# Gated delta rule and mixture of columns: k and q against the state in one product of 64 columns, small products in whole batches, new order on all engines

## The chip, the cores and the metric

The kernel runs on one core of a Trainium2 chip. It is one program, launched once. The metric is its time on the device in microseconds, the median of several runs. All arithmetic is in fp32.

## What is computed

Two layers follow each other on x of 4 sequences, 2048 tokens and 512 features. The first is a gated delta rule with 16 heads of width 32, which is a recurrence over the tokens:

```
S = S * a_t                                  # per head, S is 32 x 32
kv_mem = k_t S ;  delta = (v_t - kv_mem) * beta_t
S = S + outer(k_t, delta) ;  y_t = q_t S
ctx = rmsnorm(y) * norm_w * silu(gate) ;  x = x + layernorm(ctx @ Wo.T + bo)
```

q, k, v, gate, beta and alpha are projections of the normed x; q and k are normed to length 1, beta is a sigmoid. The second is a mixture: each token picks by its logits one of 16 columns (512 to 128, gelu, back to 512), and layer norms follow.

```
logits = cosine(x, col_emb) + sigmoid(gelu(x @ gate_w1 + b1) @ gate_w2 + b2)
weights = onehot(argmax(logits)) * softmax(logits)
y = (gelu(x @ W_cols + b_cols) * weights) @ proj_w + proj_b + x ;  out = x + layernorm(y)
```

## The kernel before

**Blocks and steps.** The 2048 tokens of each sequence are cut into 32 blocks of 64 tokens, and a block into two chunks of 32 (c = 0, 1). A loop of 35 steps is software pipelined and unrolled. A step makes the projections of the next block (`ahead`), the scan of this block (`chain`), output projection, norms and gate of the previous block (`after`), and routing of the one before that (`late`). Behind the loop stands the mixture itself, from 3020 us on.

**A chunk of the scan.** `state_to_u` multiplies S with the decayed k, on 64 tiles of 32 x 32 (16 groups times 4 heads), into the PSUM tile `uk`. DVE then solves a triangular system in two halves of 16 tokens: `solve_half(c, 0)`, then PE's `first_half_to_u(c)` corrects the second half, then `solve_half(c, 1)`. A solve reads products of pairs of keys times beta, 15 columns of them. Each solve ends in a transpose to `delT`. `change_state` makes the outer products into `su`, and `add_to_state` adds them to the decayed state: S is ready for the next chunk. The outputs are q times S (`state_to_outputs`) plus `chunk_to_outputs`, in the PSUM tile `uq`, copied out by ACT (`copy_outputs`). `key_products(c)` makes the products of keys and of keys with queries, and `decay_products(c)` on DVE writes them as `Ak` and `Aq`.

**Pairs.** SP writes `Ak` to DRAM (`write_rows`) and reads it back, spread over the partitions of each head, in eight transfers (`fetch_pairs(c, j)`), two of them outstanding. POOL multiplies them with beta (`pairs_times_beta(c, j)`: seven operations and then eight). The two buffers `pairs[0]`, `pairs[1]` come free when the solve of the same j is over.

**Small and large products.** On PE an fp32 matmul is two matmul instructions in the trace, so a batch of 64 small products is x128, and half a batch x64. A projection (`project`) is eight instructions for a half, 16 for the pair that fills a bank. `squares_sum`, `decays`, `turn` (transposes), `output_projection`, `gate_hidden`, `gate_logits` and `ranks` are the other large ones. All of them write one of three PSUM banks `work`. `TURNS` lists the uses in the order of PE, and `into` makes PE wait until the earlier use of the bank has been read, by the semaphore in `READ_BY`.

**Order.** The order on each engine is written by hand in its `step`; engines work in order and wait on semaphores (`take`). Routing: `choose_columns` on DVE, `ranks` on PE, `rows_of_tokens` on DVE reads the bank of `rank` and makes `slot`; POOL adds a bias to `xfw` and scatters its rows to DRAM by `slot`. Then POOL adds the residual (`x1`), DVE takes its statistics, ACT norms it into `xfw`, and PE turns that (`turn("xfT", ...)`).

## Time and profile before

| | us |
|---|---|
| median of 3 runs | 3423.63 (3423.21 to 3427.54) |
| profiled execution | 3454.87 |
| its span | 3453.1 |
| granted PE clock, mean | 0.912 of full |
| PE, DVE, POOL, ACT busy | 3006.9, 2357.6, 1913.1, 1824.4 |
| transfers, issue to landing: pairs, `pair_rows`, `xt` | 3.5 to 3.7, 2.3, 5.4 |

A timeline row has the start, the length of a merged run of equal instructions, the engine, the line, what is written and read, and the count; brackets give idle time ahead of it and what ended it. PE's rows overlap by a few hundredths, so that distances are taken from start to start. The lengths of PE's rows are modelled. "issue" is a wait for nothing that the profile shows.

### The profile page before, as it was taken

What the parts mean: (1) busy time and instruction counts of PE and PEld (TensorE: products, weight loads), DVE (VectorE), ACT (ScalarE), POOL (GpSimd) and SP (SyncE); (2) the same over time, 40 slices, a digit from 0 to 9 for tenths busy, and PEclk for the clock granted to TensorE, in tenths of its full rate; (3) what the DMA queues carried; (4) which work ended last, traced back from release to release, by engine and by line L of the source; (5) the groups of instructions that cost most, each with busy time, mean ns of one, the idle gap of its engine ahead of it and who ended that gap; (6) DMA issues with size and microseconds to landing.
All of it is one profiled execution on the core that took longest, in us unless ns stands there. A gap on an engine that the chain in (4) does not pass through costs nothing.

```text
span 3453.1 us, 141658 instructions
## 1 busy us (share of the span) xinstructions
PE 3006.9 (87%) x59368; PEld 2295.4 (66%) x59368; DVE 2357.6 (68%) x10708; ACT 1824.4 (53%) x4154; POOL 1913.1 (55%) x2903
## 2 busy tenths in 40 slices
PE   4899999999999999999999999999999999637774
PEld 4667777777777777777777777777777777414443
DVE  1667666666666766777666666666666677657896
ACT  2355555555555555555555555555555555326664
POOL 1555565455555555555565555555556555416887
PEclk9899999999999999999999999999999999759997
DMA  3544444544444445444444454444445444545773
GB/s 112 132 119 115 113 117 112 124 117 108 118 115 114 117 121 124 112 113 117 115 117 112 124 124 110 114 115 115 116 116 124 124 111 118 142 141 105 132 126 65
DMA packets 350030, 404.87 MB, mean 117 GB/s; under 512 B 31169, under 2 KB 293953, under 8 KB 348881
## 3 DMA queue, kind: packets, MB, share of 16 engines
q1 hardware_dynamic: 332752, 362.10, 42.1%
q0 software_dynamic: 16640, 33.71, 5.4%
q8 instruction: 468, 7.67, 1.0%
q14 instruction: 170, 1.38, 0.1%
HBM read 323.97 MB, written 75.93 MB: 116 GB/s over the span
## 4 chain that ended last, share of the span: by engine, by line
PE 62%; ACT 20%; DVE 11%; issue 4%; POOL 1%; ACTq 1%; DMA 1%; POOLq 0%; SPq 0%; DVEq 0%
PE work L437 25%; PE work L535 7%; PE work L543 3%; PE work L446 3%; DVE uk L1158 3%; DVE Ut L1155 3%; PE su L504 3%; PE work L454 2%; PE uq L497 2%; PE uk L477 2%; PE kkq L469 2%; PE uq L492 2%; PE work L530 2%; PE work L522 2%; PE work L511 2%
## 5 line engine op out<-in xcount | busy, mean ns | idle before, releaser
L437 PE MATMUL work<-xT,w_sb 128*128 128x256 f32 x5120 | 1314.1, 407 | 6.5 <-ACT beta L835 5.1
L992 POOL TENSOR_TENSOR pairs<-pairs,beta 128x240 f32<-128x240 f32 (+14 forms) x1920 | 862.4, 488 | 667.0 <-ACT beta L835 380.9
L437 PEld LDWEIGHTS work<-xT,w_sb 128*128 128x128 f32 x5120 | 996.3, 202 | 183.8 <-issue 31.1
L1158 DVE TENSOR_TENSOR uk<-uk,Ut 128x120 f32<-128x120 f32 (+14 forms) x3840 | 708.6, 226 | 1.1
L1155 DVE TENSOR_TENSOR Ut<-pairs,uk 128x120 f32<-128x120 f32 (+14 forms) x3840 | 688.2, 215 | 5.5 <-POOL pairs L992 5.0
L802 ACT ACTIVATE qraw<-work 128x512 f32<-128x512 f32 x128 | 75.9, 593 | 432.2 <-DVE kq L1171 305.5
L1165 DVE TENSOR_TENSOR S<-Sd,su 128x512 f32<-128x512 f32 x64 | 44.0, 687 | 359.1 <-PE su L504 359.1
L535 PE MATMUL work<-wo_sb,ctxT 128*128 128x512 f32 x512 | 240.6, 613 | 6.3 <-POOL ctxT L1011 6.3
L1003 POOL TENSOR_TENSOR kd<-kd,dec 128x512 f32<-128x512 f32 x64 | 68.0, 1084 | 258.8 <-DVE kd L1237 258.8
L492 PEld LDWEIGHTS uq<-kqd,S 32*32 32x32 f32 x8192 | 90.7, 114 | 156.8 <-ACT oT L792 105.8
L1145 DVE TENSOR_TENSOR uk<-vT,uk 128x128 f32<-128x128 f32 x256 | 62.9, 291 | 187.7 <-PE uk L485 115.8
L492 PE MATMUL uq<-kqd,S 32*32 32x32 f32 x8192 | 105.6, 203 | 95.7 <-ACT oT L792 93.4
L809 ACT ACTIVATE qr<-work 128x512 f32<-128x512 f32 x128 | 75.9, 593 | 193.9 <-PE work L446 191.5
L1017 POOL TENSOR_TENSOR xfw<-xfw,pb_sb 128x1024 f32<-128x1024 f32 x32 | 75.5, 2359 | 175.7 <-DVE slot L1224 175.7
L535 PEld LDWEIGHTS work<-wo_sb,ctxT 128*128 128x128 f32 x512 | 93.7, 193 | 105.4 <-issue 94.8
L1171 DVE TENSOR_TENSOR kq<-qraw,qr 128x512 f32<-128x512 f32 x128 | 136.1, 1082 | 35.0 <-ACT qr L810 35.0
L839 ACT ACTIVATE vT<-work 128x512 f32<-128x512 f32 x64 | 38.2, 597 | 224.5 <-PE work L437 224.5
L981 POOL TENSOR_TENSOR kqd<-kq,eg 128x1024 f32<-128x1024 f32 x64 | 150.3, 2349 | 3.8 <-DVE kq L1171 3.8
L976 POOL TENSOR_TENSOR Sd<-S,eg_end 128x512 f32<-128x512 f32 x64 | 67.9, 1061 | 148.6 <-DVE S L1165 148.6
L446 PE MATMUL work<-qsq,squares 128*128 128x512 f32 x256 | 147.0, 658 | 0.0
L469 PEld LDWEIGHTS kkq<-kq 32*32 32x32 f32 x8192 | 119.1, 105 | 34.1 <-issue 29.8
L1194 DVE TENSOR_TENSOR lt<-work,gb_sb 128x32 f32<-128x32 f32 x32 | 6.1, 191 | 195.7 <-PE work L556 195.7
(249 smaller groups left out, 5970.8 us busy)
## 6 DMA issues: line engine op xcount, KB each, us to landing
pairs<-pair_rows SPq DMA_DIRECT2D x512, 256.0 KB, 3.5
pairs<-pair_rows SPq DMA_DIRECT2D x512, 224.0 KB, 3.7
xt<-in_x SPq DMA_DIRECT2D x66, 256.0 KB, 5.4
pair_rows<-Ak SPq DMA_DIRECT2D x64, 256.0 KB, 2.3
x<-in_x SPq DMA_DIRECT2D x64, 256.0 KB, 4.8
out<-x SPq DMA_DIRECT2D x64, 256.0 KB, 3.7
wo_sb<-xs_rows SPq DMA_DIRECT2D x30, 258.0 KB, 2.9
w_sb<-in_w_in SPq DMA_DIRECT2D x1, 5120.0 KB, 14.9
```

What stands on the lines that cost most here:

```text
L437: mm = pe.matmul(w[:, half * BT:(half + 1) * BT], w_sb[:, f, j * D + hg * P:j * D + (hg + 1) * P], xT[:, f, :], start=(f == 0), stop=(f == ...
L446: pe.matmul(w, blk1, qsq[n % 2][:], start=True, stop=True).then_inc(s["ss_full"], 1)
L469: on_tiles(half, "kkq_full", lambda g, q, q_half: pe.matmul(kkq[q, g], kq[q, g, c, 0, :], kq[q, g, c].rearrange("p a t -> p (a t)"), start ...
L492: on_tiles(half, None, lambda g, q, q_half: pe.matmul(uq[q, g], S[q, g, :], kqd[c][q, g, 1, :], start=(g == 0), stop=True, skip_group_chec ...
L504: on_tiles(half, "su_full", lambda g, q, q_half: pe.matmul(su[q, g, :], kd[c][q, g, :], delT[c][q, g, :], start=True, stop=True))
L535: mm = pe.matmul(w, flat(ctxT[:, hg * B + tb * BL:hg * B + (tb + 1) * BL, :]), wo_sb[:, hg, :], start=(hg == 0), stop=(hg == KD - 1))
L543: mm = pe.matmul(w[:, n * BT:(n + 1) * BT], gw1_sb[:, f, n * P:(n + 1) * P], xfT[:, f, :], start=(f == 0), stop=(f == KD - 1))
L981: link(nc.gpsimd.tensor_tensor(kqd[c][:], kq[:, :, c], eg[:, :, c * C:(c + 1) * C].unsqueeze(2).to_broadcast([P, G, 2, C]), ALU.mult), "kq ...
L992: ins = nc.gpsimd.tensor_tensor(a, a, beta[:, :, t:t + WID[t0]], ALU.mult)
L1155: link(v.tensor_tensor(Ut[:, g, 0:n], pr[:, g], uk[:, g, at:at + 1].to_broadcast([P, G // 2, n]), ALU.mult), "vb_free" if i and (c, j, t0) ...
L1158: link(v.tensor_tensor(uk[:, g, at + 1:at + 1 + n], uk[:, g, at + 1:at + 1 + n], Ut[:, g, 0:n], ALU.subtract), f"pairs_free{j}" if i and t ...
L1171: link(v.tensor_tensor(unit(kq, hp)[:, :, :, 1 - j, :], per_chunk(qraw[n % 2][:]), per_chunk(qr[n % 2][:]), ALU.mult), "kq_ready", hold=(n ...
```

## The change

On PE, `uk` and `uq` become the two halves of one tile `u` over two banks, and `state_to_u` makes k and q times S as one product of 64 columns for each tile; `state_to_outputs` is gone. It now waits for the earlier outputs to be copied. `on_tiles` issues a whole batch of 64 products, where it was halves, and every batch has large products behind it. `chunk_to_outputs(c)` follows in the same step, behind `change_state` and a large product.

ACT takes sigmoids as tanh: the gate is copied out of PSUM, its tanh is taken later, and DVE makes (tanh + 1) times the gate (`norm_w` is halved once); beta is tanh and then an affine. Tanh and gelu share one table, and the table is loaded by hand twice a step. `length_of_normed` moves to the next step, raw q and k are copied straight into `kq`, the norm of the next tokens moves ahead. On DVE `rows_of_tokens` goes behind `solve_half(1, 0)`, the statistics of the next tokens ahead of it, and `decay_products(0)` into the middle of `solve_half(1, 1)`. On POOL `decay_state(1)` and the first seven operations of `pairs_times_beta(1, 1)` go ahead of the additions to `x1`, and the `dec` operations ahead of the scatter. SP loads the next tokens between two fetches, and stores ahead of `write_rows(0)`.

```
 TURNS = [
-    ("logits",), ("xT", 0), ("xT", 1), ("qk", 0), ("rms", 0), ("rms", 1), ("alpha",), ("qk", 1), ("ss", 0),
-    ("qk", 2), ("wo", 0), ("wo", 1), ("rank",), ("ss", 1), ("G", 0), ("G", 1), ("qk", 3), ("ss", 2),
-    ("gate", 0), ("ss", 3), ("gate", 1), ("beta", 0), ("beta", 1), ("xfT", 0), ("xfT", 1), ("v", 0), ("v", 1),
-    ("hid",),
+    ("xT", 0), ("xT", 1), ("rms", 0), ("rms", 1), ("logits",), ("qk", 0), ("qk", 1), ("ss", 0), ("qk", 2), ("ss", 1),
+    ("G", 0), ("G", 1), ("wo", 0), ("wo", 1), ("rank",), ("ss", 2), ("qk", 3), ("gate", 0), ("ss", 3), ("gate", 1),
+    ("beta", 0), ("beta", 1), ("xfT", 0), ("xfT", 1), ("v", 0), ("hid",), ("v", 1),
 ]
 BANK = {use: n % NW for n, use in enumerate(TURNS)}
+BANK["alpha",] = BANK["logits",]
 READ_BY = dict(xT="xT_ready", qk="q_sq_ready", ss="ss_read", alpha="alpha_read", rms="rms_read", G="eg_ready", wo="wo_read",
-               rank="rank_read", gate="gate_used", beta="beta_ready", v="v_read", xfT="xfT_ready", hid="h_ready",
+               rank="rank_read", gate="gate_read", beta="beta_read", v="v_read", xfT="xfT_ready", hid="h_ready",
                logits="logits_read")
...
         qsq = [sb(f"qsq{n}", [P, GU * T]) for n in range(2)]
-        qr = [sb(f"qr{n}", [P, GU * T]) for n in range(2)]
-        sg = sb("sg", [P, GU * T])
+        qr = [sb(f"qr{n}", [P, GU * T]) for n in range(4)]
...
-        uk = ps("uk", [P, G, C])
-        uq = ps("uq", [P, G, C])
+        u = ps("u", [P, G, 2, C])
+        uk, uq = u[:, :, 0, :], u[:, :, 1, :]
...
+                if ahead:
+                    load_tokens(following)
+                if chain:
                     fetch_pairs(1, 1)
-                if ahead:
-                    load_tokens(following)
+                if after:
+                    store(block)
+                if ahead:
                     write_rows(0)
-                if after:
-                    store(block)
-                if ahead:
                     fetch_pairs(0, 0)
...
+            def key_products(c):
+
+                take(pe, "A_ready", free=1, use="kkq")
+                on_tiles(lambda g, q, q_half: pe.matmul(
+                    kkq[q, g], kq[q, g, c, 0, :], kq[q, g, c].rearrange("p a t -> p (a t)"), start=True, stop=True))\
+                    .then_inc(s["kkq_full"], 1)
+
+            def state_to_u(c):
+
+                take(pe, "kqd_ready")
+                take(pe, "uq_free", free=1)
+                take(pe, "S_ready")
+                on_tiles(lambda g, q, q_half: pe.matmul(
+                    u[q, g].rearrange("p a t -> p (a t)"), S[q, g, :], kqd[c][q, g].rearrange("p a t -> p (a t)"),
+                    start=(g % (G // 2) == 0), stop=True, skip_group_check=True)).then_inc(s["uk_full"], 1)
+
...
-                on_tiles(half, None, lambda g, q, q_half: pe.matmul(
-                    uq[q, g], S[q, g, :], kqd[c][q, g, 1, :], start=(g == 0), stop=True, skip_group_check=True))
...
                 if chain:
-                    state_to_u(1, 0)
-                if ahead:
+                    change_state(0)
+                if after:
+                    take(pe, "ctx_ready", 2)
+                    output_projection(0)
+                if chain:
+                    chunk_to_outputs(0)
+                if after:
+                    output_projection(1)
+                if chain:
+                    state_to_u(1)
+                if late:
+                    ranks()
+                if ahead:
...
                     project("gate", 4, 0, 0)
-                if chain:
-                    chunk_to_outputs(0, 0)
-                if ahead:
+                    project("gate", 4, 0, 1)
                     squares_sum(3)
-                    project("gate", 4, 0, 1)
-                if chain:
-                    chunk_to_outputs(0, 1)
-                if ahead:
                     project("gate", 4, 1, 0)
                     project("gate", 4, 1, 1)
...
                 if after:
                     take(pe, "xf_ready", TB)
                     turn("xfT", xfw, 0)
...
+            def load_tanh_gelu():
+                nc.scalar.preload_act_table_set("gelu_and_others")
...
-                take(act, "kq_ready", free=2)
+                j, hp = divmod(n, 2)
                 take(act, "qk_full")
-                nc.scalar.activation(qraw[n % 2][:], bank("qk", n), ACT.Copy)
+                nc.scalar.activation(unit(kq, hp)[:, :, :, 1 - j, :], per_chunk(bank("qk", n)), ACT.Copy)
...
+            def copy_gate(p, hp):
+
+                take(act, "gate_full")
+                link(nc.scalar.activation(flat(unit(silu[1 - p], hp)), bank("gate", hp), ACT.Copy), "gate_read", hold=True)
+
+            def gate_tanh(p, hp):
+
+                nc.scalar.activation(gate_t[hp], flat(unit(silu[1 - p], hp)), ACT.Tanh, scale=0.5).then_inc(s["gate_ready"], 1)
+
+            def beta_sigmoid(hp):
+
+                b = flat(unit(beta, hp))
+                take(act, "beta_full")
+                link(nc.scalar.activation(b, bank("beta", hp), ACT.Tanh, scale=0.5), "beta_read", hold=True)
+                link(nc.scalar.activation(b, b, ACT.Identity, scale=0.5, bias=half[:]), "beta_ready")
...
+                    copy_gate(p, 1)
+                    take(act, "x_mv_ready")
+                    token_norm(x_rn, x_mv)
+                    norm_tokens(xn, xt, x_rn, "xn_ready")
                 if after:
                     take(act, "x1_mv_ready")
                     token_norm(x1_rn, x1_mv)
                     norm_tokens(xfw, x1, x1_rn, "xf_ready")
...
+                load_tanh_gelu()
                 if ahead:
                     if chain:
                         take(act, "vb_free")
-                    link(sigmoid("beta", 0, flat(unit(beta, 0))), "beta_ready")
-                    link(sigmoid("beta", 1, flat(unit(beta, 1))), "beta_ready")
+                        take(act, "pr_ready", 8)
+                    beta_sigmoid(0)
+                    gate_tanh(p, 0)
+                    gate_tanh(p, 1)
+                    beta_sigmoid(1)
+                if after:
+                    copy_turned("xfT", xfT, 0)
+                    copy_turned("xfT", xfT, 1)
+                if ahead:
                     copy_values(0)
...
                 load_ln_exp()
+                if chain:
+                    copy_outputs(1)
+                if ahead:
+                    take(act, "gate_used", 2)
+                if chain:
+                    square_outputs(0)
+                    square_outputs(1)
                 if ahead:
                     copy_values(1)
-                    take(act, "x_mv_ready")
...
+            def pairs_times_beta(c, j, parts=(0, 1)):
+
+                for n in parts:
...
+                if ahead:
+                    for hp in range(2):
+                        take(pool, "gT_ready")
+                        d = flat(unit(dec, hp))
+                        link(nc.gpsimd.tensor_tensor(d, d, gT[hp], ALU.subtract))
+                        by_chunk = d.rearrange("p (n t) -> p n t", t=C)
+                        link(nc.gpsimd.tensor_tensor(by_chunk, by_chunk, mask[:].unsqueeze(1).to_broadcast([P, GU * NC, C]), ALU.add),
+                             "diff_ready")
...
+                if chain:
+                    decay_state(p, 1)
+                    pairs_times_beta(1, 1, (0,))
                 if late:
                     pool.wait_ge(s["scat_done"], added)
...
                 if chain:
-                    decay_state(p, 1)
-                    pairs_times_beta(1, 1)
+                    pairs_times_beta(1, 1, (1,))
...
-                    link(v.tensor_tensor(uk[:, g, h], uk[:, g, h], beta[:, g, th], ALU.mult), behind=1)
+                for i, g in enumerate(turns):
+                    link(v.tensor_tensor(uk[:, g, h], uk[:, g, h], beta[:, g, th], ALU.mult),
+                         "vb_free" if i and (c, j) == (NC - 1, 1) else None, behind=1, hold=True)
 
                 for t0 in range(CS - 1):
+                    if t0 in between:
+                        between[t0]()
                     if t0 in PARTS:
                         take(dve, "pr_ready")
...
                     solve_half(0, 0)
                     decay_products(1)
-                    for c in range(NC):
-                        link(v.transpose(kd[c][:], kq[:, :, c, 0, :]), "kt_ready")
+                if after:
...
                     take(dve, "corr_full")
                     solve_half(0, 1)
+                if ahead:
+                    scale(0)
                 if late:
                     choose_columns()
-                if ahead:
-                    take(dve, "kqd_ready", 2, free=2)
...
+                    for hp in range(2):
+                        take(dve, "g_copied")
+                        link(v.transpose(gT[hp], flat(unit(dec, hp))), "gT_ready")
                 if late:
                     weigh_columns()
                 if after:
...
                     token_stats(y, y_mv, 1, "y_mv_ready")
+                if chain:
+                    take(dve, "uk_full")
+                    solve_half(1, 0)
                 if late:
                     rows_of_tokens()
-                if chain:
-                    add_to_state()
                 if ahead:
                     scale(1)
-                    take(dve, "g_copied")
-                    link(v.transpose(gT[0], gsb[0]), "gT_ready")
-                    take(dve, "g_copied")
-                    link(v.transpose(gT[1], gsb[1]), "gT_ready")
-                if chain:
-                    take(dve, "uk_full")
-                    solve_half(1, 0)
-                if ahead:
                     scale(2)
                     scale(3)
-                    take(dve, "gate_ready")
-                    link(v.tensor_tensor(flat(unit(silu[1 - p], 0)), bank("gate", 0), sg[:], ALU.mult), "gate_used")
                 if after:
                     for tb in range(TB):
                         take(dve, "x1_ready")
                         token_stats(x1, x1_mv, tb, "x1_mv_ready")
                 if ahead:
                     take(dve, "dec_ready", 2)
+                if chain:
+                    take(dve, "corr_full")
+                    solve_half(1, 1, {PARTS[1]: lambda: decay_products(0)} if ahead else {})
+                elif ahead:
                     decay_products(0)
```

Order on PE, in a full step around the second `state_to_u` (L477 before, L474 now). Before:

```order
L446 MATMUL work<-qsq,squares 128x512 [waits wo_read,q_sq_ready]
L522 MATMUL work<-squares,xt 128x128 [waits wo_read,lax_ready]
L522 MATMUL work<-squares,xt 128x128 x3
L522 MATMUL work<-squares,xt 128x128 [waits rank_read]
L522 MATMUL work<-squares,xt 128x128 x3
L477 MATMUL uk<-kqd,S 32x32 [waits S_ready,kqd_ready]
L477 MATMUL uk<-kqd,S 32x32 x31
L437 MATMUL work<-xT,w_sb 128x256 [waits ss_read]
L437 MATMUL work<-xT,w_sb 128x256 x3
L477 MATMUL uk<-kqd,S 32x32 x32
L437 MATMUL work<-xT,w_sb 128x256 x4
```

Now:

```order
L474 MATMUL u<-kqd,S 32x64 [waits S_ready,uq_free,kqd_ready]
L474 MATMUL u<-kqd,S 32x64 x63
L558 MATMUL work<-ohs,squares 128x32 [waits eg_ready,oh_ready]
L561 MATMUL work<-ohs,squares 128x16
L564 MATMUL work<-ohs,squares 128x16 x2
L444 MATMUL work<-qsq,squares 128x512 [waits wo_read,q_sq_ready]
L435 MATMUL work<-xT,w_sb 128x256 [waits wo_read]
L435 MATMUL work<-xT,w_sb 128x256 x7
L435 MATMUL work<-xT,w_sb 128x256 [waits rank_read]
L435 MATMUL work<-xT,w_sb 128x256 x7
```

Before, two half batches had a projection between them, and `ranks` stood ahead. Now the batch is whole and 64 columns wide; `ranks` and a sum of squares follow, and the second projection behind them (the gate) waits for `rank_read`, which comes from `rows_of_tokens` on DVE.

Order on DVE around `rows_of_tokens` (its five rows begin with `lt<-work,rows`). Before:

```order
L1219 TENSOR_TENSOR lt<-work,rows 128x32 [waits rank_full]
L1221 TENSOR_TENSOR rows<-rows,work 128x16 [waits dve_step]
L1222 TENSOR_TENSOR lt<-lt,oh 128x32
L1223 TENSOR_REDUCE slotf<-lt 128x2 [waits dve_step]
L1224 CAST slot<-slotf 128x2 [waits dve_step]
L1165 TENSOR_TENSOR S<-Sd,su 128x512 [waits Sd_ready,su_full]
L1171 TENSOR_TENSOR kq<-qraw,qr 128x16x32 [waits q_r_ready]
L1271 STREAM_TRANSPOSE qraw<-qsq 128x512 [waits g_copied,kq_ready]
L1273 STREAM_TRANSPOSE ctxT<-ctxT 128x512 [waits g_copied]
L1145 TENSOR_TENSOR uk<-vT,uk 128x8x16 [waits uk_full]
```

Now:

```order
L1145 STREAM_TRANSPOSE delT<-u 128x512 [waits pairs_free0]
L1215 TENSOR_TENSOR lt<-work,rows 128x32 [waits rank_full]
L1217 TENSOR_TENSOR rows<-rows,work 128x16 [waits dve_step]
L1218 TENSOR_TENSOR lt<-lt,oh 128x32
L1219 TENSOR_REDUCE slotf<-lt 128x2 [waits dve_step]
L1220 CAST slot<-slotf 128x2 [waits dve_step]
L1156 TENSOR_TENSOR kq<-kq,qr 128x16x32 [waits q_r_ready] x3
L1103 BN_STATS stats<-x 128x6 [waits x1_ready]
L1104 BN_AGGR x_mv<-stats 128x2 [waits dve_step]
L1103 BN_STATS stats<-x 128x6 [waits x1_ready,dve_step]
L1104 BN_AGGR x_mv<-stats 128x2 [waits dve_step]
L1127 TENSOR_TENSOR u<-vT,u 128x8x16 [waits corr_full,dec_ready]
```

Before, the slots came ahead of the update of S, and so ahead of the solve that begins with `uk<-vT,uk`. Now they come behind that solve's last transpose, and the statistics of `x1` and `solve_half(1, 1)` behind them.

Order on POOL from the wait for the slots. Before:

```order
L1017 TENSOR_TENSOR xfw<-xfw,pb_sb 128x2x512 [waits slot_ready]
L1019 DMA xs_rows<-xfw,slot 67712x516 [waits pool_step]
L1019 DMA xs_rows<-xfw,slot 67712x516
L1025 TENSOR_TENSOR dec<-qsq,qraw 128x512 [waits gT_ready]
L1027 TENSOR_TENSOR dec<-dec,mask 128x512 [waits pool_step]
L1030 TENSOR_TENSOR dec<-ctxT 128x512 [waits gT_ready]
L1032 TENSOR_TENSOR dec<-dec,mask 128x512 [waits pool_step]
L1039 TENSOR_TENSOR x<-x,y 128x512 [waits zn_ready,xres_loaded,scat_done]
L1039 TENSOR_TENSOR x<-x,y 128x512 [waits zn_ready]
L976 TENSOR_TENSOR Sd<-S,eg_end 128x512 [waits S_ready]
L992 TENSOR_TENSOR pairs<-pairs,beta 128x16x15 [waits pairs_in101,pairs_in100]
```

Now:

```order
L1008 TENSOR_TENSOR xfw<-xfw,pb_sb 128x2x512 [waits slot_ready]
L1010 DMA xs_rows<-xfw,slot 67712x516 [waits pool_step]
L1010 DMA xs_rows<-xfw,slot 67712x516
L959 TENSOR_TENSOR Sd<-S,eg_end 128x512 [waits S_ready]
L975 TENSOR_TENSOR pairs<-pairs,beta 128x16x15 [waits pairs_in101,pairs_in100]
L975 TENSOR_TENSOR pairs<-pairs,beta 128x16x14
L975 TENSOR_TENSOR pairs<-pairs,beta 128x16x13
L975 TENSOR_TENSOR pairs<-pairs,beta 128x16x12
L975 TENSOR_TENSOR pairs<-pairs,beta 128x16x11
L975 TENSOR_TENSOR pairs<-pairs,beta 128x16x10
L975 TENSOR_TENSOR pairs<-pairs,beta 128x16x9
L1022 TENSOR_TENSOR x<-x,y 128x512 [waits zn_ready,xres_loaded,scat_done]
```

The two additions `x<-x,y` stood ahead of `Sd` and of the pair products; now `Sd` and seven pair products stand between the scatter and them.

## Rows read from the trace of the kernel before

**Rows 1.** The page, busy time of each engine (share of the span) and instructions.
```profile
PE 3006.9 (87%) x59368; PEld 2295.4 (66%) x59368; DVE 2357.6 (68%) x10708; ACT 1824.4 (53%) x4154; POOL 1913.1 (55%) x2903
```

**Rows 2.** One line's instructions, L1165: duration in ns, first and last start.
```profile
L1165 DVE TENSOR_TENSOR S<-Sd,su x64: 669/687/689, 127.1 to 3015.0; 128x512 f32<-128x512 f32 x64
```

**Rows 3.** Timeline of PE, 1500 to 1610: start, length (us), line, operation [idle before <-releaser].
```profile
1506.24 0.41 PE L565 MATMUL work<-ohs,squares 128*128 128x32 f32 x2
...
1507.16 1.10 PE L446 MATMUL work<-qsq,squares 128*128 128x512 f32 x2
...
1523.22 3.72 PE L437 MATMUL work<-xT,w_sb 128*128 128x256 f32 x16
...
1541.34 1.08 PE L492 MATMUL uq<-kqd,S 32*32 32x32 f32 x64 [2.94 <-ACT oT L792]
1543.88 1.12 PE L454 MATMUL work<-squares,xfw 128*128 128x128 f32 x4 [1.46 <-ACT beta L835]
1544.79 3.23 PE L437 MATMUL work<-xT,w_sb 128*128 128x256 f32 x8
...
1559.22 0.75 PE L477 MATMUL uk<-kqd,S 32*32 32x32 f32 x64
...
1563.06 1.07 PE L553 MATMUL work<-ceT,xfT 128*128 128x16 f32 x8 [0.96 <-issue]
...
1569.10 0.38 PE L497 MATMUL uq<-Aq,delT 32*32 32x32 f32 x21 [1.20 <-issue]
...
1573.06 1.99 PE L469 MATMUL kkq<-kq 32*32 32x64 f32 x128
...
1606.02 0.44 PE L477 MATMUL uk<-kqd,S 32*32 32x32 f32 x23 [0.48 <-issue]
1606.39 1.99 PE L437 MATMUL work<-xT,w_sb 128*128 128x256 f32 x8
```

**Rows 4.** Waits of PE in the whole run: us in total, times, longest.
```profile
PE uq L492 <- ACT oT L792: 93.4, 31, 3.4
...
PE uk L477 <- issue: 26.0, 52, 1.7
```

**Rows 5.** Timeline of PE in the last step, which has no projections.
```profile
2950.06 2.12 PE L469 MATMUL kkq<-kq 32*32 32x64 f32 x78 [2.43 <-issue]
```

**Rows 6.** Timeline of DVE, 1500 to 1610.
```profile
1507.64 0.16 DVE L1219 TENSOR_TENSOR lt<-work,rows 128x32 f32<-128x32 f32 x1
...
1582.80 0.49 DVE L1145 TENSOR_TENSOR uk<-vT,uk 128x128 f32<-128x128 f32 x2 [1.27 <-PE uk L485]
...
1592.07 0.72 DVE L1160 STREAM_TRANSPOSE delT<-uk 128x512 f32<-128x512 f32 x1
```

**Rows 7.** Timeline of POOL, 1500 to 1600.
```profile
1508.61 2.35 POOL L1017 TENSOR_TENSOR xfw<-xfw,pb_sb 128x1024 f32<-128x1024 f32 x1 [5.63 <-DVE slot L1224]
...
1513.70 1.28 POOL L1025 TENSOR_TENSOR dec<-qsq,qraw 128x512 f32<-128x512 f32 x1
...
1518.88 2.51 POOL L1039 TENSOR_TENSOR x<-x,y 128x512 f32<-128x512 f32 x2
1521.34 1.06 POOL L976 TENSOR_TENSOR Sd<-S,eg_end 128x512 f32<-128x512 f32 x1
...
1544.39 3.99 POOL L992 TENSOR_TENSOR pairs<-pairs,beta 128x240 f32<-128x240 f32 x7 [12.38 <-ACT beta L835]
```

**Rows 8.** Timeline of ACT, 1500 to 1600.
```profile
1541.94 1.28 ACT L835 ACT_TABLE_LOAD   x1
1543.23 1.09 ACT L835 ACTIVATE beta<-work 128x512 f32<-128x512 f32 x2
...
1559.82 0.29 ACT L771 ACTIVATE nsc<-x_mv,eps 128x2 f32<-128x2 f32 x1
...
1562.61 1.52 ACT L752 ACTIVATE xn<-xt,x_rn 128x512 f32<-128x512 f32 x2
```

**Rows 9.** Timeline of SP, the DMA queue of the transfers, 1500 to 1600.
```profile
1534.10 27.92 SPq L342 DMA_DIRECT2D pairs<-pair_rows  x16
```

More of the change, by code:

```diff
@@ L376, in step @@
                 if ahead:
+                    write_rows(0)
                     fetch_pairs(0, 0)
@@ L489, in state_to_outputs @@
-            def state_to_outputs(c, half):
-                if not half:
-                    take(pe, "uq_free", free=1)
-                on_tiles(half, None, lambda g, q, q_half: pe.matmul(
-                    uq[q, g], S[q, g, :], kqd[c][q, g, 1, :], start=(g == 0), stop=True, skip_group_check=True))
-            def chunk_to_outputs(c, half):
-                on_tiles(half, "o_full", lambda g, q, q_half: pe.matmul(
-                    uq[q, g], delT[c][q, g, :], Aq[c][q, g, :], start=False, stop=True, skip_group_check=True))
@@ L670, in step @@
                     turn("xfT", xfw, 0)
-                if ahead:
-                    project("beta", 3, 1, 1)
-                if chain:
-                    state_to_outputs(1, 0)
-                if after:
                     turn("xfT", xfw, 1)
```

279 lines of the change are left out of this document (109 added, 170 removed).

## The prediction

> **What bounds the kernel now.** I read the busy times first, then one step of the scan by engine, then the waits. PE is busy for 87% of the span [rows 1], and the scan takes most of it: 64 chunk updates of S start between 127.1 and 3015.0 us [rows 2], so a step of two chunks lasts (3015.0 - 127.1) / 31.5 = 91.7 us. The reader is to see in [rows 3] that PE works through nearly all of a step. From `state_to_u(0)` at 1559.22 to the row behind `state_to_u(1)` at 1606.39 it loses only three pauses called issue (0.96, 1.20, 0.48). The other loss is at 1541.34: 2.94 us waiting for `oT`, 1.46 at 1543.88, and then a product of eight matmuls that takes 3.23 us instead of half of 3.72, or 1.4 more, since the granted clock was at its half level there. The waits of the whole run say that this recurs: 93.4 us over 31 steps for `oT`, 26.0 us of issue before `state_to_u` [rows 4]. So a step is PE work, and one knot of some 6 us on ACT.
>
> **The change, part by part.** I walk one full step of the new order, t = 0 where PE starts `state_to_u(0)`.
>
> *PE to the end of `state_to_u(1)`.* The old stretch is 1606.39 - 1559.22 = 47.2 [rows 3]; without its three pauses 44.5. Out of it move `chunk_to_outputs(1)` (two half batches of 0.7, 1.4), `ranks` (1507.16 - 1506.24 = 0.9) and half a projection (1.9); `chunk_to_outputs(0)` comes in (1.4): 41.7. `state_to_outputs(0)` goes (1.4) and two products grow from 32 to 64 columns. A whole batch of 64 columns took 1.99 (the 128 matmuls at 1573.06), two halves of 32 columns 1.4: 2 x 0.55 = 1.1 more, so 41.4. Seven small runs fewer: a large product between small ones takes 1.9 where half of a pair takes 1.85, and each small run has a similar edge, together about 0.15 a run by these rows, so 1.0 less: 40.4. In the other stretch the second `state_to_outputs` goes likewise. For the whole step the same count is 91.7, less 4.4 of the ACT waits, 1.9 at the half clock (1.4, and 0.5 on the small work beside it) and 1.1 of issue, less 2.8 for both `state_to_outputs`, plus 1.1 of columns, less 1.8 of edges for 12 runs: 80.8 of PE work. The issue pauses remain, as each batch has some 2 to 11 us of large products behind it (the rival below says otherwise). I put 0.7 in this stretch, by the 26 us / 31 = 0.8 of [rows 4]. PE is at t = 41.1, and DVE, which has sums, turns and three token statistics to do first, starts `solve_half(1, 0)` at X = 41.3.
>
> Here the Trainium skill has a rule (TensorE: Matmul & The Clock Gate, "Back-to-back issue gap"): a matmul of 1 to 64 columns has one price. By it the merged product would cost what one of 32 columns does, and a step would be 1.1 us shorter. The trace does not agree: 1.99 for 64 columns against 1.4 for two halves of 32 [rows 3].
>
> *A new chain through four engines.* What decides lies behind X. In the new order `rows_of_tokens` on DVE stands behind `solve_half(1, 0)`, and the slots that it makes release POOL. On POOL stand behind them, in this order, the addition to `xfw` and two scatters, `decay_state(1)`, the first half of `pairs_times_beta(1, 1)`, and only then the two additions that make `x1`. Before, the slots were made ahead of the solve. The prices:
> - solve 1592.07 + 0.72 - 1582.80 = 10.0, slots 1508.61 - 1507.64 = 1.0 [rows 6];
> - `xfw` and scatters 1513.70 - 1508.61 = 5.1, `Sd` 1.0, seven pair products 4.0, `x1` 2.5 [rows 7];
> - statistics of the second half of `x1` 0.9, as a BN pair.
> So `x1`'s statistics are there at X + 24.5 = 65.8. ACT needs them for the norm that PE's turn of `xf` waits for. ACT is itself at work until 66.5: PE may start `gate(0)` only when the bank of `rank` has been read, at X + 10.4 = 51.7, though it arrives there at 41.1 + 0.9 + 1.0 + 3.7 = 46.7. It idles 5 us, runs at the half clock for a while (1.5, from the 1.4 above), and `gate(0)`, a sum of squares and `gate(1)` end at 61.6; then a copy of 0.6 and the norm of the next tokens, 4.3 [rows 8]. From 66.5: norm 4.3 (1562.61 + 1.52 - 1559.82), table 1.3, and tanh and the affine of `beta(0)`, two gate tanhs, tanh of `beta(1)`: 5 x 0.55 = 2.7 [rows 8]. The bank of `beta(1)` is free at 74.8, and only then may PE start `v(0)`. PE would have been there at 51.7 + 1.5 + 3.7 + 1.0 + 3.7 + 1.4 + 3.7 + 2.0 + 3.7 + 1.9 = 74.3, so the two ways meet within half a microsecond: the wait for `rank` costs no more than the chain does.
>
> *The rest of the step*: `v(0)` 3.7, `change_state(1)` 1.4, hidden 3.7, `chunk_to_outputs(1)` 1.4, `v(1)` 3.7 = 13.9, with 0.3 of issue and 0.3 for scatters that land late: 89.3. `delT` is ready at 65.8 + 10.0 + 1.4 for `decay_products(0)` = 77.2, before PE's `change_state(1)` at 78.5.
>
> *What is hidden.* ACT gains four activations (2.4 us) and loses six of eight table loads of 1.28 (7.7); it saves the knot at 1541. That copy of the outputs now stands early, behind `chunk_to_outputs(0)`, and has 3 us until PE wants the bank. The copy of raw q and k straight into `kq`, and the product in place, cost what the rows of the same size do; they lie behind PE. Bounds for the unseen: the new forms (tanh, a strided copy, a stride of 64 in u) between 0 and +0.1 us each on about 10 of the path, 0 to +1 a step; I take 0. The pair transfers: 16 took 27.92 us to issue [rows 9], 1.75 each. Rows of chunk 0 are written at t = 72 + 2; both halves land by t = 88.7 and POOL has them at 91.2, wanted by DVE at 96.8. Cover 5 us. The next fetch ends at +18, then rows, then eight more, then the tokens at t = 31 to 36, wanted at 38. Cover 2 us, and this is the thin one: transfers 15% slower would cost 1 to 3 us a step.
>
> **Sum.** 91.7 - 89.3 = 2.4 us a step, 31 steps: 74. Start, last step and the tail after 3015 do the same work. The profiled execution took 3454.9 us, 0.9% above the median of 3423.6 of the runs: 3381 profiled, or 3350 us as the median.
>
> **Rivals.**
> 1. *PE alone sets the step.* If the chain from X is much shorter than I add up, 80.8 of work and 1.1 of issue remain, 81.9: 9.8 us a step, 304 in all, 3454.9 - 304 = 3151, about 3122 as the median. For it: every number of the chain is an end-to-end difference with some queueing in it. Against: the order of POOL is fixed, and its 12.6 us behind the slots can't shrink.
> 2. *Nothing gained, a late transfer.* The tokens or the pairs come 1 to 3 us late, since SP now issues tokens between two fetches; the step is 91 to 92, the time 3400 to 3430. For it: cover of 2 us. Against: a step has some 58 us of pair transfers at that rate, so that SP has room, and what is late in one step is not added to in the next.
> 3. *Slower: whole small batches starve.* In the last step, where no projections stand between, PE stops for 2.43 us in the middle of a whole batch [rows 5]. The new order has ten whole batches a step where the old had two, and of these two one had the pause of 1.20 at 1569.10 [rows 3]. The place is `change_state(1)` to `state_to_u(1)`, eight batches in which PE is the bound; one pause of 2.4 us a step there uses up the whole gain, two make 94.1 and 3454.9 + 74 = 3529, or 3497 as the median; 1.2 at each of the eight would make 98.9. Against: the other whole batch, of 64 columns, ran through at 1573.06, and the long pauses stand where small work follows small work, with 24 matmuls of logits and the turns at most between.
> The Trainium skill (Runtime: NRT & Kernel Launch, "Instruction fetch mechanics") says that fetch is mostly hidden, which would leave this rival no chance; the pauses of [rows 5] speak against that, though no row proves that they are fetch.
>
> **How the numbers follow.** Forecast 0.52 (its own range 3315 to 3390), rival 1 0.13, rival 2 0.15, rival 3 0.20. What this kernel's measurement can tell from no change is about 0.2%, 7 us. Faster: 0.52 + 0.13 + 0.6 of rival 2 + a little of a single short pause = 0.77; within: 0.06; slower 0.17. The range runs from 3290 (a chain 2 us shorter than mine, below it only rival 1) to 3430 (rival 2 whole, not two pauses of rival 3).
>
> **What would show it.** Right: PE idle of about 5 us a step before the gate projection, ended by DVE's `rows`; hardly any idle before `state_to_u`'s S; ACT's two table loads a step; the half clock behind the rank wait; POOL waiting for the slots some 10 us longer than now; a step of 89.3. Wrong: a PE idle of over 2 us called issue inside a u product (rival 3), DVE waiting for `xt` (rival 2), a step under 86 or over 92.

## The result, and the profile after

The changed kernel takes 3466.69 us (median of 4 runs, 3453.52 to 3474.05), the kernel before on the same chip 3425.59 (3423.21 to 3430.67): a ratio of 1.0114, 95% interval 1.0079 to 1.0149. The forecast was 3350. Measured again on another chip it is 3465.03 against 3453.40, 1.003 (1.001 to 1.005); there it is the kernel before that takes another time. So the change makes the kernel 0.3 to 1.1% slower. Ratios below are to the kernel before on the chip of the run.

The page of the changed kernel, busy times as in [rows 1], with 8192 matmuls fewer on PE:
```profile
PE 2887.7 (83%) x51176; PEld 2252.4 (65%) x51176; DVE 2583.5 (74%) x10710; ACT 1662.8 (48%) x4105; POOL 1913.3 (55%) x2903
```
PE has 119 us less work, and the time isn't shorter. DVE is busy for 226 us more with two instructions more: something on DVE takes longer than it did. The updates of S, beside [rows 2]:
```profile
L1150 DVE TENSOR_TENSOR S<-Sd,su x64: 686/687/689, 125.6 to 3024.8; 128x512 f32<-128x512 f32 x64
```
From first to last they take 2899.2 us, before 2887.9. From the second update to the 62nd are 30 full steps: 92.5 us each, before 92.2 (the 91.7 of the prediction is the mean with the short last step in it). That last step takes 83.6, before 75.8. From the last update to the end are 443.5 us, before 438.1.

The waits of PE, as in [rows 4] (us in total, times, longest):
```profile
PE work L435 <- DVE rows L1217: 151.6, 29, 6.5
...
PE work L435 <- ACT beta L807: 48.9, 32, 1.6
PE work L452 <- ACT xfw L713: 47.2, 30, 16.6
PE work L452 <- ACT beta L807: 36.6, 30, 1.3
...
PE u L474 <- issue: 17.7, 19, 2.4
```
The wait for `oT` is gone. In its place is the one forecast for the bank of `rank`, 5.2 us in each of 29 steps. One step on PE, from `state_to_u(0)` to the next (columns as in [rows 3]):
```profile
1562.97 1.99 PE L474 MATMUL u<-kqd,S 32*32 32x64 f32 x128
...
1599.06 1.99 PE L474 MATMUL u<-kqd,S 32*32 32x64 f32 x128
...
1603.66 3.62 PE L435 MATMUL work<-xT,w_sb 128*128 128x256 f32 x16
1612.01 6.33 PE L435 MATMUL work<-xT,w_sb 128*128 128x256 f32 x16 [4.73 <-DVE rows L1217]
...
1633.99 0.66 PE L452 MATMUL work<-squares,xfw 128*128 128x128 f32 x4 [0.48 <-ACT xfw L713]
1635.90 0.66 PE L452 MATMUL work<-squares,xfw 128*128 128x128 f32 x4 [1.25 <-ACT beta L807]
1638.18 5.20 PE L435 MATMUL work<-xT,w_sb 128*128 128x256 f32 x16 [1.62 <-ACT beta L807]
...
1653.04 1.99 PE L474 MATMUL u<-kqd,S 32*32 32x64 f32 x128
```
The merged product is one unbroken run of 1.99, and `state_to_u(1)` ends at t = 38.1, not 41.1. Behind the rank wait and behind the wait for `beta` a projection takes 6.33 and 5.20 us instead of 3.7: the mean granted clock is 0.57 and 0.70 of full there, so the half level holds for most of the first and part of the second. Over the whole profiled execution it is 0.909. The step shown is a quick one: as the median of the full steps `state_to_u(1)` ends at t = 39.7.

DVE in the same step, beside [rows 6]; `rows` and the slots stand behind the solve:
```profile
1601.72 0.46 DVE L1127 TENSOR_TENSOR u<-vT,u 128x128 f32<-128x128 f32 x2
...
1610.95 0.72 DVE L1145 STREAM_TRANSPOSE delT<-u 128x512 f32<-128x512 f32 x1
...
1612.31 0.17 DVE L1220 CAST slot<-slotf 128x2 int32<-128x2 f32 x1
1612.39 3.44 DVE L1156 TENSOR_TENSOR kq<-kq,qr 128x512 f32<-128x512 f32 x2
...
1620.58 7.23 DVE L1156 TENSOR_TENSOR kq<-kq,qr 128x512 f32<-128x512 f32 x1 [4.76 <-ACT qr L771]
1627.74 0.68 DVE L1103 BATCH_NORM_STATS2 stats<-x 128x6 f32<-128x512 f32 x1
1628.67 0.69 DVE L1103 BATCH_NORM_STATS2 stats<-x 128x6 f32<-128x512 f32 x1
```
POOL over the same time, beside [rows 7]:
```profile
1612.56 2.72 POOL L1008 TENSOR_TENSOR xfw<-xfw,pb_sb 128x1024 f32<-128x1024 f32 x1 [9.79 <-DVE slot L1220]
1615.55 1.17 POOL L1010 DMA_INDIRECT xs_rows<-xfw,slot  x1 [0.28 <-POOL xfw L1008]
1617.02 0.99 POOL L1010 DMA_INDIRECT xs_rows<-xfw,slot  x1 [0.30 <-issue]
1618.04 1.07 POOL L959 TENSOR_TENSOR Sd<-S,eg_end 128x512 f32<-128x512 f32 x1
1619.06 4.00 POOL L975 TENSOR_TENSOR pairs<-pairs,beta 128x240 f32<-128x240 f32 x7
1623.03 2.48 POOL L1022 TENSOR_TENSOR x<-x,y 128x512 f32<-128x512 f32 x2
1625.48 2.92 POOL L975 TENSOR_TENSOR pairs<-pairs,beta 128x128 f32<-128x128 f32 x8
1628.36 2.35 POOL L964 TENSOR_TENSOR kqd<-kq,eg 128x1024 f32<-128x1024 f32 x1
```
POOL does what was forecast at the time forecast: `x1` is ready at 1625.5, X + 23.8. But DVE is inside a product of the size 128x512 that began at 1620.58 and ends at 1627.8. Until 1628.36 POOL is never idle for more than 0.3 us. The product doesn't wait for a pause of POOL, though. It ends inside one of POOL's last pair products, which takes 0.73 us with it, where the next and smaller one takes 0.26:
```profile
1627.23 0.73 POOL L975 TENSOR_TENSOR pairs<-pairs,beta 128x48 f32<-128x48 f32 x1
```
So it is in 27 of the 32 fourth products: they end 0.58 to 0.68 us after the start of POOL's pair product of 128x48 or 128x32, and 11 to 14 POOL operations, the one they began in included, end before that. The statistics of `x1` are done at 1629.6, and ACT waits for them, beside [rows 8]:
```profile
1629.62 0.29 ACT L732 ACTIVATE nsc<-x_mv,eps 128x2 f32<-128x2 f32 x1 [1.98 <-DVE x_mv L1104]
...
1632.42 1.52 ACT L713 ACTIVATE xfw<-x,x_rn 128x512 f32<-128x512 f32 x2
1633.96 1.28 ACT L708 ACT_TABLE_LOAD   x1
1635.25 0.60 ACT L807 ACTIVATE beta<-work 128x512 f32<-128x512 f32 x1
```
All of these products of the run in one line, and behind it those of the kernel before (duration ns: shortest, median, longest):
```profile
L1156 DVE TENSOR_TENSOR kq<-kq,qr x128: 648/1076/8305, 61.1 to 2917.3; 128x512 f32<-128x512 f32 x128
```
```profile
L1171 DVE TENSOR_TENSOR kq<-qraw,qr x128: 647/1002/2147, 57.9 to 2906.7; 128x512 f32<-128x512 f32 x128
```
The medians hardly differ, the longest do. Taken by their place in the step the four of the changed kernel have medians of 0.72, 0.68, 2.84 and 7.56 us, those before 0.68, 1.72, 0.82 and 1.05. In all 346 us against 136, most of what DVE gained in busy time.

### The profile page after: what moved, and what is told of

Its sections match the earlier page's. It is cut to its first block, busy times and chain, and to the rows that moved or that the text cites. A ratio compares the mean times of both kernels' runs of the same rounds, so it can differ in the third digit from the quotient of the medians.

```text
span 3468.3 us, 125046 instructions
## 1 busy us (share of the span) xinstructions
PE 2887.7 (83%) x51176; PEld 2252.4 (65%) x51176; DVE 2583.5 (74%) x10710; ACT 1662.8 (48%) x4105; POOL 1913.3 (55%) x2903
## 4 chain that ended last, share of the span: by engine, by line
PE 53%; DVE 26%; ACT 11%; issue 4%; DMA 2%; POOL 1%; ACTq 1%; SPq 0%; DVEq 0%; POOLq 0%
PE work L435 23%; DVE kq L1156 6%; DVE u L1143 5%; DVE Ut L1140 5%; PE work L528 5%; PE work L536 3%; DVE stats L1103 3%; PE u L474 3%; PE work L444 2%; PE su L496 2%; PE u L677 2%; PE kkq L465 2%; PE work L504 2%; PE u L488 2%; DMA pairs<-pair_rows 1%
## 5 line engine op out<-in xcount | busy, mean ns | idle before, releaser
L435 PE MATMUL work<-xT,w_sb 128*128 128x256 f32 x5120 | 1327.8, 418 | 201.5 <-DVE rows L1217 151.6
L975 POOL TENSOR_TENSOR pairs<-pairs,beta 128x240 f32<-128x240 f32 (+14 forms) x1920 | 870.4, 489 | 936.8 <-DMA pairs<-pair_rows 936.7
L435 PEld LDWEIGHTS work<-xT,w_sb 128*128 128x128 f32 x5120 | 1061.6, 211 | 433.9 <-DVE rows L1217 163.2
L1143 DVE TENSOR_TENSOR u<-u,Ut 128x120 f32<-128x120 f32 (+14 forms) x3840 | 708.8, 226 | 0.0
L1140 DVE TENSOR_TENSOR Ut<-pairs,u 128x120 f32<-128x120 f32 (+14 forms) x3840 | 689.1, 216 | 3.7 <-POOL pairs L975 2.4
L1156 DVE TENSOR_TENSOR kq<-kq,qr 128x512 f32<-128x512 f32 x128 | 346.0, 2724 | 137.3 <-ACT qr L771 137.3
L763 ACT ACTIVATE kq<-work 128x512 f32<-128x512 f32 x128 | 75.9, 593 | 263.0 <-PE work L435 262.9
L677 PEld LDWEIGHTS u<-kq,xfT 128*128 128x128 f32 x640 | 89.3, 214 | 139.1 <-ACT kq L922 138.8
L677 PE MATMUL u<-kq,xfT 128*128 128x128 f32 x640 | 104.2, 312 | 70.9 <-ACT kq L922 70.9
L474 PEld LDWEIGHTS u<-kqd,S 32*32 32x32 f32 x8192 | 121.2, 106 | 55.6 <-issue 55.5
L474 PE MATMUL u<-kqd,S 32*32 32x64 f32 x8192 | 135.0, 216 | 17.9 <-issue 17.7
L465 PE MATMUL kkq<-kq 32*32 32x64 f32 x8192 | 132.4, 219 | 20.8 <-DVE kq L1156 19.9
L797 ACT ACTIVATE silu<-work 128x512 f32<-128x512 f32 x64 | 38.1, 596 | 208.4 <-PE work L435 208.4
```

Of the source, the lines that this page charges most:

```text
L435: mm = pe.matmul(w[:, half * BT:(half + 1) * BT], w_sb[:, f, j * D + hg * P:j * D + (hg + 1) * P], xT[:, f, :], start=(f == 0), stop=(f == ...
L465: on_tiles(lambda g, q, q_half: pe.matmul(kkq[q, g], kq[q, g, c, 0, :], kq[q, g, c].rearrange("p a t -> p (a t)"), start=True, stop=True))\
L474: on_tiles(lambda g, q, q_half: pe.matmul(u[q, g].rearrange("p a t -> p (a t)"), S[q, g, :], kqd[c][q, g].rearrange("p a t -> p (a t)"), s ...
L677: mm = pe.matmul(m_hp[m % 2], wcur[m % 2][:, f, :], xsT[m % 2][:, f, :], start=(f == 0), stop=(f == KD - 1))
L975: ins = nc.gpsimd.tensor_tensor(a, a, beta[:, :, t:t + WID[t0]], ALU.mult)
L1140: link(v.tensor_tensor(Ut[:, g, 0:n], pr[:, g], uk[:, g, at:at + 1].to_broadcast([P, G // 2, n]), ALU.mult), behind=1)
```

## The experiments

Medians below that are counted from X, the start of `solve_half(1, 0)` as in the prediction, are over 29 full steps of a run.

Theory A: what holds the step is the chain that starts at the slots, and it is 3 us longer than forecast since the fourth product on DVE is held while POOL works without a gap. Rivals: the product is slow for its own form (B), or PE's or ACT's order is the limit, whatever DVE does.

### The fourth product early: e1
PE sums the fourth squares ahead of the gate projection, and ACT makes their norm ahead of the gate's copy, so the product comes before POOL's run.
```diff
@@ PE @@
+                    squares_sum(3)
                     project("gate", 4, 0, 0)
                     project("gate", 4, 0, 1)
-                    squares_sum(3)
@@ ACT @@
-                    copy_gate(p, 0)
                     inverse_norm(3)
+                    copy_gate(p, 0)
```


> The kernel with the change, but PE makes the sum of squares of k, second half (squares_sum(3)), before the gate product that waits for rank, and ACT its inverse norm before the gate copy. Theory A (the fourth product kq*qr on DVE arrives while POOL runs without a pause, and waits for 7 us where it used to take 1; the statistics of x1, and with them ACT's norm and PE's v product, come 3 us late): the fourth product now stands right behind the third, in the time of POOL's scatters, takes under 2 us, and a step is some 3 us shorter: 3370 to 3390 us. Theory B (the waits for rank and the half clock behind them cost the time, the product on DVE is beside the path): 3440 to 3470.

Measured: 3375.09 us, ratio 0.9778 (0.9760 to 0.9795). A full step takes 89.25. The product in one step of it, and all of them:
```profile
1575.39 0.76 DVE L1156 TENSOR_TENSOR kq<-kq,qr 128x512 f32<-128x512 f32 x1 [3.73 <-ACT qr L771]
```
```profile
L1156 DVE TENSOR_TENSOR kq<-kq,qr x128: 649/684/2857, 61.3 to 2820.7; 128x512 f32<-128x512 f32 x128
```
With the held product gone the step is what the prediction summed up for it, 89.3. The statistics of `x1` are done at X + 24.8 instead of X + 27.9 (medians). The net gain is 3.2 us a step, 90 us against e11. It has other parts too: `v(0)` runs at the full clock again (median 3.72 us for 6.18), X itself comes 2.2 us later in the step (42.1 for 39.9), and DVE waits 45.2 us in total for tokens, where the change has 11.1. The edit also moves a sum of squares on PE ahead of the rank wait, so that e1 alone doesn't part theory A from the order on PE or ACT; e8 below takes the held product away by another edit and has nearly the same gain. The last step stays at 83.5.

### Another form of the product: e3
The fourth product reads its raw values from a tile of its own with unit stride, not in place from `kq`. ACT then has to wait for the product before it norms the next tokens into that tile.
```diff
-                nc.scalar.activation(unit(kq, hp)[:, :, :, 1 - j, :], per_chunk(bank("qk", n)), ACT.Copy)
+                nc.scalar.activation(xn[:, 0, :] if n == 3 else unit(kq, hp)[:, :, :, 1 - j, :],
+                                     bank("qk", n) if n == 3 else per_chunk(bank("qk", n)), ACT.Copy)
...
+                raw = per_chunk(xn[:, 0, :]) if n == 3 else unit(kq, hp)[:, :, :, 1 - j, :]
```


> The kernel with the change, but the raw copy behind the fourth product kq*qr goes to a contiguous tile (xn), so that this product is not in place and reads no strided operand; ACT makes the decays of pairs before that copy, and waits for the product before it norms the next tokens. Theory A (the product waits for a pause of POOL, whatever its operands): it still takes 6 to 8 us and the time is 3460 to 3540, as ACT's norm now waits for it. Rival D (the form in place with strides of 64 is what is slow): it takes about 1 us and the time is 3370 to 3400.

Measured: 3474.81 us, 1.0055 (1.0036 to 1.0074), no gain. The product alone:
```profile
L1159 DVE TENSOR_TENSOR kq<-xn,qr x32: 685/7516/8374, 75.5 to 2923.0; 128x512 f32<-128x512 f32 x32
```
The form changes nothing. B is refuted.

### POOL waits for the product: e5
```diff
+                if ahead:
+                    pool.wait_ge(s["kq_ready"], seen[pool, "kq_ready", ""] + 4)
                 if chain:
                     decay_state(p, 1)
```


> The kernel with the change, and POOL waits for the fourth product kq*qr before decay_state(1) and its seven pair products, so that the product meets a POOL at rest. Theory A: the product falls from 7.5 to 0.7 us; POOL starts some 2 us later than now, the statistics of x1 come about 1 us earlier, a step gets 0 to 2 us shorter, 3400 to 3470 us on a chip where the kernel before takes 3425. Rival D (the product is slow by itself): it stays at 7 us, POOL is 7 us later, and the time goes up by over 100 us.

Measured: 3469.37 us, 1.0111 (1.0089 to 1.0133). The same product at the same place in the step, and POOL's new wait:
```profile
1525.49 0.69 DVE L1158 TENSOR_TENSOR kq<-kq,qr 128x512 f32<-128x512 f32 x1 [3.83 <-ACT qr L771]
```
```profile
POOL Sd L959 <- DVE kq L1158: 101.0, 31, 13.2
```
This shows why the product is long: nothing about it has changed but that POOL stands still, and 7.5 us become 0.7. The time does not follow, since POOL's 3.3 us a step now stand in the same chain: `x1` is ready at X + 26.3 instead of X + 23.8, its statistics at X + 27.3 instead of X + 27.9 (medians), and a step still takes 92.5. What pays is to move the product, not to make POOL wait for it.

### The slots ahead of the solve: e2, e4, e8
e2 moves `ranks` on PE and `rows_of_tokens` on DVE to where they cut both the rank wait and the head of the chain:
```diff
@@ PE @@
                     chunk_to_outputs(0)
+                if late:
+                    ranks()
...
-                if late:
-                    ranks()
@@ DVE @@
+                if late:
+                    rows_of_tokens()
                 if after:
                     output_rows(1)
...
-                if late:
-                    rows_of_tokens()
```


> The kernel with the change, but ranks on PE stands behind chunk_to_outputs(0) and rows_of_tokens on DVE before solve_half(1, 0), so that slots and the bank of rank come 10 us earlier. Theories A and B both hold the chain from the slots for the bound: no wait of 5 us for rank, POOL's scatter and x1 about 10 us earlier, step 83 to 86, 3200 to 3290 us. Rival C (a step is bound elsewhere, by the pair transfers or by the sum of PE work and pauses, and the wait for rank only fills up slack): 3400 to 3470.

Measured: 3191.84 us, 0.9242 (0.9230 to 0.9253), against both kernels the faster. A full step takes 84.0 us, the last 75.3, and no wait of PE for `rows` is among its larger ones. The page:
```profile
PE 2802.4 (88%) x51176; PEld 2198.9 (69%) x51176; DVE 2429.8 (76%) x10710; ACT 1654.5 (52%) x4105; POOL 1914.4 (60%) x2903
```
The step is 8.5 us shorter than in the change, and comes near rival 1's 81.9. e4 makes the edits of e1 and e2 together:

> e1 and e2 together. If the chain from the slots is the bound, the first removes the fourth product's wait and the second the wait for rank; step 82 to 85, 3180 to 3270 us, no slower than e2 alone. If e2 alone already leaves PE as the bound, both are the same within 0.3%.

Measured: 3201.61 us, 0.9268 (0.9242 to 0.9294), no better than e2 alone: with the slots early the fourth product is not held any more (median 0.75 us in e2), so the edit of e1 has nothing to take away. e8 parts e2 in two: the ranks, and the reading of their bank, come early, the slots stay behind the solve.
```diff
+                if late:
+                    read_ranks()
                 if after:
                     output_rows(1)
...
                     solve_half(1, 0)
                 if late:
                     rows_of_tokens()
```


> The kernel with the change, but only the two reads of the bank of rank on DVE (and ranks on PE) stand before solve_half(1, 0); the three operations that make the slots stay behind it. The wait of 5 us for rank and the half clock behind it go, POOL's chain starts where it did. Theory A (the chain from the slots over POOL, x1 and ACT bounds the step): the fourth product comes early enough to stand behind the third, so the gain is that of e1, 2 to 3.5%, and PE idles 8 to 10 us ahead of the turn of xf and the v product instead. Theory B (the wait for rank bounds it): the gain is near that of e2, 7 to 9%.

Measured: 3394.14 us, 0.9895 (0.9878 to 0.9911), a step of 89.6. The rank wait is away and PE waits for the chain instead, in the whole run and in one step:
```profile
PE work L452 <- ACT xfw L713: 220.1, 31, 17.2
```
```profile
1587.08 1.12 PE L452 MATMUL work<-squares,xfw 128*128 128x128 f32 x4 [6.25 <-ACT xfw L713]
...
1591.26 6.24 PE L435 MATMUL work<-xT,w_sb 128*128 128x256 f32 x16 [1.16 <-ACT beta L807]
```
PE idles about as long as in the change (there 151.6 us for `rank` and 47.2 for `xfw`): the wait was not the cause, it was the slack that the chain left. The 2.9 us don't come from the wait either. Without the wait the gate projection ends earlier, so the fourth product comes before POOL's run, and none of the four takes more than 2.9 us:
```profile
L1156 DVE TENSOR_TENSOR kq<-kq,qr x128: 647/684/2854, 61.4 to 2826.0; 128x512 f32<-128x512 f32 x128
```
The fourth has a median of 0.68, the statistics of `x1` are done at X + 24.5, and from X to the next step it is 48.9 us instead of 52.4 (medians), 3.4 less, which is what the statistics gain. The order on ACT is that of the change. So this is the gain of e1 over again, as theory A expected, and of the 8.5 us of e2 the other 5.6 (89.6 - 84.0) come with the slots.

### One product or two: e6, e10, e11
e6 is e2 with the 64-column product taken back to two of 32, in the same place, one behind the other:
```diff
-                on_tiles(lambda g, q, q_half: pe.matmul(
-                    u[q, g].rearrange("p a t -> p (a t)"), S[q, g, :], kqd[c][q, g].rearrange("p a t -> p (a t)"),
...
+                for a, tile in enumerate((uk, uq)):
+                    mm = on_tiles(lambda g, q, q_half: pe.matmul(
+                        tile[q, g], S[q, g, :], kqd[c][q, g, a, :],
...
```


> The kernel of e2, with the product of 64 columns undone: in the same place PE makes 64 products of k and then 64 of q with 32 columns each, into the same tile. By the rows of the kernel before (1.4 us for 64 tiles of 32 columns, 1.95 for 64 columns) a chunk costs PE 0.8 us more, 1.6 a step, and 256 instructions more stand together: if PE bounds e2, 50 us slower than e2 (up to 100 with pauses in the supply of instructions), 1.5 to 3%. If merging is hidden, under 10 us.

Measured: 3433.73 us, 0.9983 (0.9954 to 1.0012), 8% above e2 where 1.5 to 3% were expected; a step takes 90.9. The columns are the same number, so the time is elsewhere:
```profile
PE u L475 <- issue: 173.5, 83, 3.9
```
```profile
1585.01 1.25 PE L475 MATMUL u<-kqd,S 32*32 32x32 f32 x125
1587.92 1.27 PE L475 MATMUL u<-kqd,S 32*32 32x32 f32 x128 [1.66 <-issue]
1591.94 0.32 PE L475 MATMUL u<-kqd,S 32*32 32x32 f32 x3 [2.75 <-issue]
```
PE stops in the middle of 256 small matmuls, with nothing that the profile shows it to wait for. These pauses are 5.6 us a step, more than the work of one of the products. e2 has few:
```profile
1552.57 1.42 PE L474 MATMUL u<-kqd,S 32*32 32x64 f32 x87
1554.96 0.80 PE L474 MATMUL u<-kqd,S 32*32 32x64 f32 x41 [0.97 <-issue]
```
e10 makes the same edit in the change as it stands, and e11 is the change, unaltered, on the same chip.

> The kernel with the change, but its product of 64 columns undone as in e6: 64 products of k and then 64 of q, of 32 columns each. Both places stand in the stretch in which PE sets the pace also here (end of a step to state_to_u(1)), so the loss should be near e6's against e2, 8 us a step: 3640 to 3760 us where the change takes 3470. If instead the slack behind the slots hides it, the loss is under 100 us.

> The kernel with the change, unaltered, on the chip of e10, as the measure for it: 1.005 to 1.015 of the kernel before.

Measured: e10 3684.19 us, 1.0657 (1.0600 to 1.0715), a step of 98.9; e11 3465.03, 1.003 (1.001 to 1.005), a step of 92.7. So the merged product is worth 219 us, 6%, against two products that stand one behind the other, and the new order with such a pair would be slower than the kernel before by about as much. Against two products kept apart by large ones, as in the kernel before, no run shows what it is worth. PE's pauses in e10 are those of e6:
```profile
PE u L475 <- issue: 174.4, 82, 4.3
```

### The second product early too: e9
```diff
@@ DVE, against e2 @@
                     scale(0)
+                    scale(1)
...
-                    scale(1)
                     scale(2)
```


> The kernel of e2, with the second product kq*qr right behind the first, ahead of solve_half(1, 0). In e2 it meets POOL's addition to xfw and waits 2.8 to 4.7 us. If DVE is near the path there, 0.5 to 1.5 us a step shorter than e2; if e2 is bound by PE, the same within 0.3%, or up to 0.5% slower as the solve starts 0.7 us later.

Measured: 3166.57 us, 0.9222 (0.9206 to 0.9238), a step of 83.3. Its interval overlaps that of e2, so the two aren't told apart, though it has the lowest time of all. The wait moved: the second product takes 1 us, the third has a median of 3.5.

## Why the prediction was wrong

**The step that failed** is the sentence "the product in place, cost what the rows of the same size do; they lie behind PE". The chain from X has no term for the fourth product: I took it as covered. It takes 7.5 us, and lies not behind PE but in the chain, between ACT's `q_r` and DVE's statistics of `x1`. The trace of before held a sign of it for whoever laid DVE beside POOL: of the products some took up to 2147 ns, with a median of 1002. I summed POOL's queue and DVE's apart, as if neither could hold the other. The Trainium skill has the rule (SBUF — State Buffer, "SBUF: two separate sides"): a pair of ports is shared by VectorE and GpSimd, and a VectorE operation with two inputs in SBUF and a GpSimd operation that reads SBUF shut each other out, the later one waiting for the whole instruction of the first. This agrees with the third product, 2.84 us against 2.72 of POOL's addition to `xfw`. For the fourth it falls short: by the rule the product would get in behind one POOL operation, the longest of which here is 1.3, but 11 to 14 of them end first, and it gets in between two of the last.

**What it cost.** Chain: `x1`'s statistics at X + 27.9 (1629.6 - 1601.72) instead of X + 24.5. The other links came out as summed: solve 9.95 for 10.0, `x1` on POOL at X + 23.8. That is 3.4 a step. e1, which takes it away, has 89.25 for the forecast 89.3, but that close an agreement is luck: it has errors of both signs in it, as the terms that follow show.

**PE's stretch**, forecast 41.1, is 38.1 in the step shown and 39.7 as the median, and X, forecast 41.3, is 38.8 and 39.9. So the chain starts 1.4 us earlier in the median step, which hid a part of the loss. Half clock: forecast 1.5 once, in truth 2.2 behind the rank wait (median 5.95 against 3.72) and 2.5 more on `v(0)` (median 6.18); I had no second one. From X to the next step it is 52.4 where I had 48.0 (89.3 - 41.3): the 3.4 of the product and the 2.5 of the second half clock are more than the difference, so the rest of the links took some 1.5 less than summed. The step shown above is 90.1, one of the shorter; two steps from 2205 on take 92.1 and 91.7, with 5.65, 6.23, 6.13 and 6.69 for these products.

**The rank wait** was right in place, cause and size (5.0 forecast, 5.2), as was "costs no more than the chain does": e8 takes it away, PE waits for `xfw` instead, and the 2.9 gained are those of the fourth product. What I didn't weigh was the order that causes both.

**Hidden work.** The table loads and the knot at `oT` went as forecast. POOL's wait for pair transfers grew from 286.0 to 936.7 us in total, but DVE waited for its pairs 2.4 us in all: the cover held.

**The rivals.** 1, PE alone: not in the change, but nearly in e2 (84.0 for 81.9), once the slots are early. 2, a late transfer: the time is above its range, and DVE waits for tokens only 11.1 us in five places. The cover was thin all the same: in e1 and e2 these waits are 45.2 and 41.0 us. 3, whole small batches starve: it did not happen in the change; issue pauses before the small products add up to about 39 us, before about 44. Its mechanism is real, though: 128 in a row mostly pass, 256 stop for 5.6 us a step. So the prediction had the sign of the merge right, and left out what it spares. From columns and edges it is worth a few us a step at most; measured against two products in a row, 7.1 a step in e10 against e11's 92.7 by their whole times, 6.2 by their steps.

**What stays open.** The last step, 83.6 against 75.8, which I took as equal: e2, e4 and e9 give it back (75.3, 75.1, 74.7), e1 and e8 don't (83.5, 84.0), so that the place of the slots decides it, not that of the ranks; which wait it is stays open. Open too is what the 5.6 us that come with the slots consist of. The 5 us more behind the last update were not settled. "Start, last step and the tail do the same work" was thus wrong by some 13 us, less 6 at the start (the first update of a full step comes that much earlier).

## What to carry to other kernels

Add up a chain over several engines with the neighbours of each link in view: an operation on VectorE with two inputs in SBUF may not have a fixed price while GpSimd works through a row of operations without a gap. Put it ahead of that row; making GpSimd wait only moved the cost here. And where an engine waits behind a new order, ask first what a chain's head waits for: moving the ranks and the slots ahead of one solve was worth 8% here. Taking away the visible wait alone gave a third of that, and this third was the held product, not the wait.

## What was not expected of the hardware

- The product of 128x512 with both inputs in SBUF took up to 8.3 us beside an unbroken run of some 14 GpSimd operations of 0.3 to 1.3 us, with its raw input strided or not, and 0.7 with GpSimd at rest. It got in near the end of the run, between two operations and without a pause of GpSimd. In the kernel before, the third and fourth products mostly begin beside such pair products too and get in behind the first one, with medians of 0.82 and 1.05. What decides between the two, these traces do not show.
- 256 small matmuls without large ones between them stopped once or twice in 63 of the 64 batches of e6, half of the stops taking 1.8 to 2.6 us; of 64 batches of 128 in e2 52 ran through. That the cause is the supply of instructions is argued from the count, not shown.
- A projection of 16 matmuls behind 5 us of idle PE took mostly 5.4 to 6.6 us instead of 3.7, at a mean granted clock of 0.57 in the one shown. So this wait of 5.2 us cost 2.2 more behind it, in the median.
